# Routing of a GNN–attention–experts layer in four single steps, with the graph rows in one operation

## The reference, cut to what matters

```python
xn = layernorm(x)                                   # x: 6250 x 256
x = x + gnn(xn, edges, ...) + mix(xn, ...)          # graph rows + linear attention
def ffn(f):                                         # f = layernorm(x), 6 experts, 256 wide
    rh = relu(f @ router_w1 + router_b1)            # router, 128 wide
    p = softmax(rh @ router_w2 + router_b2)
    top_w, top_i = top_k(p, 2)
    rw = softmax(top_w)                             # two weights a row
    # three dense layers of each of the two chosen experts, weighted by rw and added
    ...
x = x + ffn(layernorm(x))
```

## Time and profile before

| | us |
|---|---|
| median of 3 runs | 745.61 (744.7 to 746.4) |
| the profiled execution | 744.4 |
| its span, first to last instruction | 742.6 |
| busy: TensorE / VectorE / ScalarE / GpSimd | 666.2 / 555.0 / 446.1 / 449.4 |

### The profile page before, as it was taken

The page is one execution under the profiler, slowest core; times in us unless marked ns, Lnnn a source line. Parts: engine busy times, 40 slices in busy tenths (PEclk is TensorE's granted clock), DMA queues, the critical chain, the costliest instruction groups (busy, mean ns, idle before and its releaser), DMA issues.

```text
span 742.6 us, 15734 instructions
## 1 busy us (share of the span) xinstructions
PE 666.2 (90%) x4705; PEld 615.6 (83%) x4705; DVE 555.0 (75%) x1427; ACT 446.1 (60%) x879; POOL 449.4 (61%) x392
## 2 busy tenths in 40 slices
PE   3999999999999988988874299999999999999993
PEld 2888888888888777867663289999999999999993
DVE  5785788888888787678777167777777777777773
ACT  2666577777777547567771166566566566656651
POOL 3465788766666200535466478888888865555555
PEclk9999999999999999899985599999999999999998
DMA  8954544444443367768554578666646965554443
GB/s 229 270 159 145 164 130 125 129 123 122 123 125 110 111 226 241 238 212 267 186 137 115 142 201 187 133 122 119 111 83 108 173 112 95 88 94 60 46 46 36
DMA packets 80759, 104.79 MB, mean 141 GB/s; under 512 B 21156, under 2 KB 62456, under 8 KB 80679
## 3 DMA queue, kind: packets, MB, share of 16 engines
q1 hardware_dynamic: 48135, 70.98, 32.2%
q0 software_dynamic: 32544, 32.80, 25.3%
HBM read 53.35 MB, written 52.26 MB: 142 GB/s over the span
## 4 chain that ended last, share of the span: by engine, by line
PE 79%; DVE 10%; ACT 3%; POOL 2%; issue 2%; DMA 2%; SPq 1%; POOLq 0%; DVEq 0%; ACTq 0%
PE kv_ps L1359 10%; PE kv_ps L1360 10%; PE kv_ps L1361 10%; PE pt L1351 6%; PE d_ps L1223 6%; PE kv_ps L1200 5%; PE kv_ps L1203 5%; PE kv_ps L1201 5%; PE xt_ps L1351 3%; PE kv_ps L1300 2%; PE pt L1200 2%; PE pt L1203 2%; PE pt L1201 2%; POOL tab L588 1%; PE pt L1291 1%
## 5 line engine op out<-in xcount | busy, mean ns | idle before, releaser
L1359 PE MATMUL kv_ps<-we_h,now_h 128*128 x648 | 192.7, 297 | 3.6 <-DVE now_l L1170 2.0
L1360 PE MATMUL kv_ps<-we_l,now_h 128*128 x648 | 183.5, 283 | 0.0
L1361 PE MATMUL kv_ps<-we_h,now_l 128*128 x648 | 183.5, 283 | 0.0
L1359 PEld LDWEIGHTS kv_ps<-we_h,now_h 128*128 128x128 f32 x648 | 124.2, 192 | 5.0 <-issue 5.0
L1360 PEld LDWEIGHTS kv_ps<-we_l,now_h 128*128 128x128 f32 x648 | 124.5, 192 | 0.0
L1361 PEld LDWEIGHTS kv_ps<-we_h,now_l 128*128 128x128 f32 x648 | 124.0, 191 | 0.0
L1150 DVE TENSOR_TENSOR work<-kv_ps,be 128x256 f32<-128x256 f32 x216 | 81.5, 419 | 50.5 <-PE kv_ps L1361 50.1
L610 POOL DMA_INDIRECT out_x<-work,arena x56 | 87.6, 1565 | 39.7 <-DVE work L1158 26.9
L790 ACT ACTIVATE now_h<-pt 128x512 fp32r<-128x512 f32 x54 | 32.5, 602 | 103.3 <-PE pt L1351 103.3
L556 POOL DMA_INDIRECT alg<-xt_tab,src_all x50 | 63.1, 1261 | 38.9 <-DVE arena L939 17.4
L962 DVE TENSOR_REDUCE ss<-xring 125x16 f32<-125x1040 f32 x50 | 61.8, 1236 | 19.9 <-ACT xring L675 18.3
(11 more groups left out here) (253 smaller groups left out, 1826.4 us busy)
## 6 DMA issues: line engine op xcount, KB each, us to landing
arena<-tab SPq DMA_DIRECT2D x80, 131.0 KB, 3.1
xring<-in_x SPq DMA_DIRECT2D x29, 224.0 KB
we_h<-wt_h SPq DMA_DIRECT2D x6, 768.0 KB, 6.0
we_l<-wt_l SPq DMA_DIRECT2D x6, 768.0 KB, 8.6
xt_tab<-arena SPq DMA_DIRECT2D x7, 577.5 KB
weight_in<-tab SPq DMA_DIRECT2D x28, 131.0 KB, 2.6
out_x<-arena SPq DMA_DIRECT2D x12, 224.0 KB
staged<-in_ew SPq DMA_DIRECT2D x9, 256.0 KB, 4.6
```

Source lines behind the costliest of these rows:

```text
L1359: pe.matmul(outp, hi[:, c, :], we_h[:, w], start=c == 0, stop=False)
L1360: pe.matmul(outp, hi[:, c, :], we_l[:, w], start=False, stop=False)
L1361: last = pe.matmul(outp, lo[:, c, :], we_h[:, w], start=False, stop=c == KC - 1)
```

## The change

Seen from the start of a group's part 0 (step s; `STARTS` = 5, 10, 14, 18, 21, 24, 27):

- The first choice is taken from the shifted logits in part 0 instead of from the probabilities in part 1: its maximum is the one that is there already, and the comparison and the multiplication with the order of the experts are one operation.
- Part 1 (s + 1) works on the exponentials without dividing them: sum, first choice taken out, reciprocal of the sum, maximum, and the difference of the two probabilities as (max - 1) times the reciprocal.
- Part 2 (s + 2, formerly s + 1) has the second choice and the running count.
- Part 3 (s + 3, formerly s + 2) has places and base. The last group starts one step later, at 27 instead of 26.
- The weights leave part 3 (`weights_of`). For groups 0 to 4 the second exponential stands beside the first one of the next group, and the weights come one step after it and raise `row_ready`. For groups 5 and 6 part 3 raises it.
- `graph_rows` is one operation on both tiles.
- The loops of TensorE, ScalarE and VectorE run to `LAST` = 31 instead of 29.

```diff
@@ -1,6 +1,7 @@
 import concourse.bass as bass
 from concourse import mybir
 from contextlib import ExitStack
+import itertools
 
 FP32 = mybir.dt.float32
 FP32R = mybir.dt.float32r
@@ -58,9 +59,12 @@
 LW = KC * F
 EW = 3 * LW
 ROUNDS = 3 * E
-AL_STEPS, R_STEPS = 6, 21
-ROUTE_STEPS = (0, 1, 9, 15)
-ROUTE = {end - 1: g for g, end in enumerate(ENDS)}
+AL_STEPS, R_STEPS = 6, 18
+LATE = 5
+STARTS = list(itertools.accumulate((end + 1 for end in ENDS), lambda last, own: max(own, last + 3)))
+ROUTE = {at: g for g, at in enumerate(STARTS)}
+SHARE = {STARTS[g + 1] if g < LATE else STARTS[g] + 1: g for g in range(GROUPS)}
+LAST = STARTS[-1] + 4
 STATS_AT = {c: max(0, -(-(CH * c - 7) // 2)) for c in range(2, CHUNKS)}
 PREP_EPS, PREP_BO, PREP_W = 1, 15, 20
 POOL_C = 17
@@ -750,18 +754,18 @@
                     relu(i - 2)
                 if 0 <= i - 1 < PR:
                     evict2(i - 1)
-                if i - 2 in ROUTE:
-                    b = ROUTE[i - 2]
+                if i in ROUTE:
+                    b = ROUTE[i]
                     n = 2 * SIZES[b]
                     act.wait_ge(lgx_ready, b + 1)
                     act.activation(lg[:, 2, 0:n, :], lg[:, 1, 0:n, :], ACT.Exp).then_inc(ex2_done, 1)
-                if i - 3 in ROUTE:
-                    b = ROUTE[i - 3]
+                if i in SHARE:
+                    b = SHARE[i]
                     n = 2 * SIZES[b]
                     act.wait_ge(d_ready, b + 1)
                     act.activation(tw[:, 5, 0:n], tw[:, 4, 0:n], ACT.Exp).then_inc(ex3_done, 1)
 
-            for i in range(PR + 4):
+            for i in range(LAST):
                 step(i)
 
 
@@ -1001,11 +1005,9 @@
                     dve.wait_ge(v_ready, T)
                 if i >= 2:
                     dve.wait_ge(x2_done, i - 1)
-                for h in range(2):
-                    last = dve.tensor_tensor(y2[i % 2][:, h, :].rearrange("p (h n) -> p h n", n=GC),
-                                             x2in[:, i % SLOTS, h, :].rearrange("p (h n) -> p h n", n=GC),
-                                             gsum[:, 2 * i + h, :].unsqueeze(1).to_broadcast([P, GH, GC]), ALU.add)
-                last.then_inc(y2_done, 1)
+                dve.tensor_tensor(y2[i % 2].rearrange("p l (h n) -> p l h n", n=GC),
+                                  x2in[:, i % SLOTS, :, :].rearrange("p l (h n) -> p l h n", n=GC),
+                                  gsum[:, 2 * i:2 * i + 2, :].unsqueeze(2).to_broadcast([P, 2, GH, GC]), ALU.add).then_inc(y2_done, 1)
 
             graph_rows(0)
             for c in range(KC):
@@ -1043,72 +1045,87 @@
                 dve.wait_ge(fin2_done, 2 * i + 1)
                 dve.scalar_tensor_tensor(row[:, :, C_NMR], mv[:, part, 0], -1.0, row[:, :, C_R], ALU.mult, ALU.mult).then_inc(fin2_done, 1)
 
+            routed = [0]
+
+            def route_link(ins):
+
+                routed[0] += 1
+                ins.then_inc(step_done, 1)
+                dve.wait_ge(step_done, routed[0])
+
+            def weights_of(b):
+
+                m = 2 * SIZES[b]
+                row = xr[b % RB][:, 0:m, :]
+                dve.wait_ge(ex3_done, b + 1)
+                route_link(dve.tensor_scalar(tw[:, 7, 0:m], tw[:, 5, 0:m], 1.0, None, ALU.add))
+                route_link(dve.reciprocal(row[:, :, C_W], tw[:, 7, 0:m]))
+                last = dve.tensor_tensor(row[:, :, C_W + 1], tw[:, 5, 0:m], row[:, :, C_W], ALU.mult)
+                if b < LATE:
+                    last.then_inc(row_ready, 1)
+
             def route(b, part):
+
                 m = 2 * SIZES[b]
                 row = xr[b % RB][:, 0:m, :]
                 lgp = lg_ps[b % 2][:, 0:m, :]
                 lg0, lg1, lg2, lg3 = [lg[:, i, 0:m, :] for i in range(4)]
                 tws = [tw[:, i, 0:m] for i in range(8)]
-                n = [b * R_STEPS + ROUTE_STEPS[part]]
-
-                def link(ins):
-                    n[0] += 1
-                    ins.then_inc(step_done, 1)
-                    dve.wait_ge(step_done, n[0])
-
-                def choose(k, prob):
-
-                    link(dve.reduce_max(tws[2 + k], prob, axis=AX.X))
-                    link(dve.tensor_tensor(lg0, prob, bc(tws[2 + k], EP), ALU.is_equal))
-                    link(dve.tensor_tensor(lg1, lg0, desc[:, :].unsqueeze(1).to_broadcast([P, m, EP]), ALU.mult))
-                    link(dve.reduce_max(tws[6], lg1, axis=AX.X))
-                    return dve.tensor_tensor(oh[:, k, :, 0:m].rearrange("p e g -> p g e"), lg1, bc(tws[6], EP), ALU.is_equal)
-
+                def first(k):
+
+                    route_link(dve.reduce_max(tws[6], lg0, axis=AX.X))
+                    return dve.tensor_tensor(oh[:, k, :, 0:m].rearrange("p e g -> p g e"), lg0, bc(tws[6], EP), ALU.is_equal)
+
+                order = desc[:, :].unsqueeze(1).to_broadcast([P, m, EP])
                 if part == 0:
                     dve.wait_ge(lg_done, 2 * ENDS[b])
-                    link(dve.reduce_max(tws[0], lgp, axis=AX.X))
+                    route_link(dve.reduce_max(tws[0], lgp, axis=AX.X))
                     dve.tensor_tensor(lg1, lgp, bc(tws[0], EP), ALU.subtract).then_inc(lgx_ready, 1)
                     dve.tensor_copy(row[:, :, C_TOK].bitcast(I32), tok_all[:, tiles_of(b)[0]:tiles_of(b)[0] + m])
+                    dve.wait_ge(lgx_ready, b + 1)
+                    route_link(dve.scalar_tensor_tensor(lg0, lg1, 0.0, order, ALU.is_ge, ALU.mult))
+                    route_link(first(0))
                 elif part == 1:
                     dve.wait_ge(ex2_done, b + 1)
-                    link(dve.reduce_sum(tws[1], lg2, axis=AX.X))
-                    link(dve.reciprocal(tws[1], tws[1]))
-                    link(dve.tensor_tensor(lg3, lg2, bc(tws[1], EP), ALU.mult))
-                    link(choose(0, lg3))
+                    route_link(dve.reduce_sum(tws[1], lg2, axis=AX.X))
+                    route_link(dve.scalar_tensor_tensor(lg3, oh[:, 0, :, 0:m].rearrange("p e g -> p g e"), -4.0, lg2, ALU.mult, ALU.add))
+                    route_link(dve.reciprocal(tws[1], tws[1]))
+                    route_link(dve.reduce_max(tws[3], lg3, axis=AX.X))
+                    dve.scalar_tensor_tensor(tws[4], tws[3], -1.0, tws[1], ALU.add, ALU.mult).then_inc(d_ready, 1)
                 elif part == 2:
-                    link(dve.scalar_tensor_tensor(lg2, oh[:, 0, :, 0:m].rearrange("p e g -> p g e"), -4.0, lg3, ALU.mult, ALU.add))
-                    link(choose(1, lg2))
-                    dve.tensor_tensor(tws[4], tws[3], tws[2], ALU.subtract).then_inc(d_ready, 1)
+                    route_link(dve.tensor_tensor(lg1, lg3, bc(tws[3], EP), ALU.is_equal))
+                    route_link(dve.tensor_tensor(lg0, lg1, order, ALU.mult))
+                    route_link(first(1))
                     dve.tensor_tensor_scan(cum[:, :, :, :].rearrange("p k e g -> p (k e g)"), carry[:, :, :].rearrange("p a g -> p (a g)"),
                                            oh[:, :, :, :].rearrange("p k e g -> p (k e g)"), 0.0, ALU.mult, ALU.add).then_inc(oh_ready, 1)
                 else:
-                    dve.wait_ge(ex3_done, b + 1)
-                    link(dve.tensor_scalar(tws[7], tws[5], 1.0, None, ALU.add))
-                    link(dve.reciprocal(row[:, :, C_W], tws[7]))
-                    dve.tensor_tensor(row[:, :, C_W + 1], tws[5], row[:, :, C_W], ALU.mult)
                     dve.wait_ge(rk_done, b + 1)
                     got = cum[:, :, :, 0:m].bitcast(FP32)
-                    link(dve.scalar_tensor_tensor(rk[:, :, :, 0:m], got, -1.0, bc(rk_ps, m), ALU.add, ALU.add))
-                    link(dve.tensor_tensor(rk[:, :, :, 0:m], rk[:, :, :, 0:m], oh[:, :, :, 0:m], ALU.mult))
-                    link(dve.reduce_sum(posf[:, :, 0:m], rk[:, :, :, 0:m].rearrange("p k e g -> p k g e"), axis=AX.X))
+                    route_link(dve.scalar_tensor_tensor(rk[:, :, :, 0:m], got, -1.0, bc(rk_ps, m), ALU.add, ALU.add))
+                    route_link(dve.tensor_tensor(rk[:, :, :, 0:m], rk[:, :, :, 0:m], oh[:, :, :, 0:m], ALU.mult))
+                    route_link(dve.reduce_sum(posf[:, :, 0:m], rk[:, :, :, 0:m].rearrange("p k e g -> p k g e"), axis=AX.X))
                     dve.tensor_copy(pos0[:, b % RB, 0:m], posf[:, 0, 0:m])
-                    dve.tensor_copy(row[:, :, C_POS].bitcast(I32), posf[:, 1, 0:m]).then_inc(row_ready, 1)
-                    link(dve.tensor_tensor(base[:, :, :], base[:, :, :], got[:, :, :, m - 1], ALU.add))
-                if part < 3:
-                    assert n[0] == b * R_STEPS + ROUTE_STEPS[part + 1], (part, n[0])
-                else:
-                    assert n[0] == (b + 1) * R_STEPS, n[0]
-
-            for i in range(PR + 4):
+                    last = dve.tensor_copy(row[:, :, C_POS].bitcast(I32), posf[:, 1, 0:m])
+                    if b >= LATE:
+                        last.then_inc(row_ready, 1)
```

(21 more changed lines are left out.)

## The result

The changed kernel takes 743.23 us (median of 20 runs, 739.1 to 746.3) and the kernel before, measured again beside it, 745.72 us (median of 20). The direction is as forecast and the time is in the range, but 7.1 us were forecast and under half of them came. In the profiled execution the span is 741.6 us against 742.6.

What follows compares the result with a forecast made beforehand. Mixing pace, routing tail and the last rows' scatters were taken to set the experts' start. The last scatter landing 7.1 us earlier cut the span from 742.6 to 735.5 us, giving a median of 738.5, range 734 to 743.5.

Steps and rivals of the forecast that it cites:

- (a): Routing on VectorE: three linked operations fewer in each group, 0.77 us saved per group.
- (b): Routing spread over VectorE's steps: part 0 takes 1.4 us, part 1 1.12, part 2 1.48, the moved weights add 0.60.
- (c): Graph rows on VectorE in one instruction: 0.07 us saved a step, only in the VectorE-bound steps.
- (d): Exponentials on ACT: 10 of 21 table loads of 1.28 us leave, but they were covered, so nothing is counted.
- (f): Rows of groups 0 to 4 ready two to four steps later: VectorE waits 0.8 us for a buffer at step 20.
- (g): GpSimd's tail: 16 scatters without a gap from 380.7, the last landing at 408.2 against 415.34, 7.1 us earlier.
- (e): Mixing pace: five routing cycles sum to 89.45 us against 100.36, 10.9 us shorter.
- rival 4: Mixing part: three smaller TensorE gaps a group lower its clock; slower, 755.5 us with six more slow steps; chance 0.08.
- below 0.8 on average from 290 to 380: Sign that the forecast is wrong: TensorE's clock averaging under 0.8 in that stretch (us) of the mixing part.
- Rival 1: Only the mixing pace binds, no buffer wait at step 20, shorter ranks step: 733 to 736 us; chance 0.16.
- Rival 2: Scatters land late: buffer waits of 2.7 us at step 20 and 1.3 at step 23, 741 to 744 us; chance 0.15.
- Rival 3: Change does nothing: VectorE's block was covered by TensorE's backlog and last rows come later, 744 to 746 us; chance 0.06.

Runs made afterwards that it cites:

- old_places: The change's shorter arithmetic and merged graph rows, all routing parts left in the steps of the kernel before: ratio to the kernel before 0.9916.
- late4_ranks: Changed kernel with group 4's weights in its own steps and group 5's ranks a step earlier, no fillers: ratio to the kernel before 0.9935.
- clk_mix_b: The same kernel as clk_mix, run again in the third set: ratio to the kernel before 0.9885.
- late4_mix: clk_mix plus group 4's weights in its own steps and group 5's ranks a step earlier: ratio to the kernel before 0.9898.
- clk_mix: Changed kernel with 5 or 8 idle TensorE matmuls (fillers) ahead of the row transposes of nine mixing steps: ratio to the kernel before 0.9893.
- clk_all: clk_mix plus 145 idle matmuls in the wait for the first expert rows and 10 before the first expert product: ratio to the kernel before 0.9918.
- clk_wait: Changed kernel with 120 idle matmuls in TensorE's wait between the last mixing product and the first expert rows: ratio to the kernel before 0.9955.

## Why the prediction was right and wrong

**Right by mechanism.** (a): five groups at 0.77 us, 3.85 us; by itself (with the merged rows) 3.65 by group 5's start in old_places, and 0.78 us a cycle in groups 1 and 2. (b): 1.34, 3.60, 3.94 and 4.20 us for 1.4, 3.59, 3.95 and 4.19. (c): 0.07 us a step was forecast, nothing is measured (0.9996), which fits. (d): the loads are covered, 1.0002; the 14 us that followed from the Trainium skill (ScalarE: Activation LUTs, What ACT_TABLE_LOAD costs) are refuted for this place: without the loads nothing moved, and a load shows 1.283 us each and no drain behind it. (f): 1.06 us for 0.8 in this execution; at full clock it is 1.45 to 2.23. In the other four executions without fillers there is none, since the late ranks of group 2 give the scatters 1.3 us more; that the forecast is met in this one hangs on group 2 being spared. (g): the tail is as worked out, no gap behind group 4's first scatter, and from group 5's first routing operation to the last scatter 25.0 us for 25.1.

**The step that failed is (e), the new cycle.** It was summed from rows at full clock, 89.45 us with a price of nothing for TensorE's clock, and the clock was set aside as rival 4, an outcome of its own with a chance of 0.08 that makes the kernel slower. It is neither: it is a term of each of the five executions without fillers. Group 5 came at 383.40 for 378.4, and 7.1 − 5.0 + 0.7 (the shorter landing) gives the 2.8 us by which the first expert product comes earlier. Of the 5.0, 3.4 are the cycles and 1.6 the later group 0; fillers give back 2.6 of the first in the mean, and 1.5 of the second, which is 1.4 us of clock in these two executions. That the rest of the sum was right shows at full clock: 89.46 to 89.50 us without the buffer wait, for 89.45. With fillers the best execution has group 5 at 378.37, and the ratio falls by 0.0065 to 0.007, 5 us, in the sets of the faster chips. The rows for it were at hand: the prediction itself quotes 0.67 behind the gap of the ranks step and a total of TensorE work of 15.6 in 18.9 us, and took the latter as an argument against. A share over a cycle doesn't tell where in it the clock is low. Of the signs named, "below 0.8 on average from 290 to 380" was not met (0.89 in both kernels), and the loss was there all the same: in 317.6 to 321.7 at 0.50. The other, a step with the ranks of over 6 us, was met, with 7.62 in group 1.

The Trainium skill's rule (TensorE: Matmul & The Clock Gate, HAM oscillation) is borne out by the rows of late4_ranks: gaps that return in every turn, and the clock down in each of the two turns shown. The price that the prediction gave it, up to 17 us, was too high: measured are 2.6 us in the cycles and some 5 us over the kernel.

**Rivals.** Rival 1 (nothing binds but the pace) did not come, but clk_mix_b comes close to its time at 737.57 us. Rival 2 (buffers back late) had its mechanism at a quarter to a half of its 4.0 us, 1.06 to 2.23 us at step 20 and nothing at step 23, and it grows as the pace does. Rival 3 holds for the spreading taken alone, with another reason: the block is shorter, and what that gives goes to the clock and to later rows.

**Left open.** What sets the clock's return after the first expert product; what idle products there are worth; why the clock fell in one execution of late4_mix with the same fillers that kept it up in clk_mix; and whether old places with fillers (0.991) or the spread order with fillers (0.9885 to 0.9929) is the better kernel, which met on one chip only.

## What to carry to other kernels

When a block on one engine is cut up and spread so that another engine has several small gaps instead of one large, price the other engine's work at its lower clock in the steps behind each gap, as a term of the sum and not as a separate outcome; here it took some 5 of 8 us, and a few idle matmuls in the gaps gave them back. Measure the arithmetic and the reordering apart: the shorter arithmetic alone, in the old places, was worth as much as the whole change or more. And where the rows become ready later, count from them to the end of the queue that they feed: 16 scatters without a gap behind group 4's rows made that queue the bound in place of the pace. Last, read more than one profiled execution: the one of the changed kernel shows one bad step of ranks, and four others show two milder ones and no buffer wait.

## What the hardware showed beyond that

- TensorE's granted clock goes to 0.50 in a step in which TensorE is busy without a pause (317.63 to 321.72), behind one in which it worked 2.59 of 4.20 us. It is the work behind the gap that pays, not the gap. Some idle products ahead of the transposes kept it at 1.00 there in clk_mix, clk_mix_b, clk_mix_c and clk_all, but not in late4_mix (0.92 over the same cycle).
- A clock that idle products had brought to 1.00 in 415 to 417.5 (clk_wait) was 0.50 when the work came at 421.4.
- The tenth scatter of group 1 in clk_mix issued at 349.04 and let VectorE go on at 357.26, some 8.2 us later, while weights load; the last scatter of the stage takes 3.77 to 5.30 us.
- The chips of the four sets took 745.5, 771.3, 746.2 and 768.7 us for the same kernel. Its mixing part hardly differs: old_places has group 5 at 384.87 on the one and on the other. The difference is in the experts' stage, 319 to 321 against 340 to 347 us from the first product on.
